# A two-layer attention kernel on one core: GELU values kept in the low half of their own slot, eight weight slots instead of six, and a start on host-transposed inputs

## The reference

```
# layer 0: only sequence 0's attention is used, and it is added to every sequence
q, k, v = x @ Wq0.T, ctx @ Wk0.T, ctx @ Wv0.T          # 16 heads
tgt2 = (softmax(q k^T / sqrt(32)) v)[0]
x = x + tgt2
# layer 1, for each of the 8 sequences
q = layer_norm(x; gq, bq) @ Wq ; k, v = layer_norm(ctx; gkv, bkv) @ Wkv
x = x + (softmax(q k^T * 32**-0.5) v) @ Wproj + bproj
x = x + gelu(layer_norm(x; gm, bm) @ W1 + b1) @ W2 + b2   # 512 -> 2048 -> 512, exact gelu
```

## Time and profile before

| what | value |
|---|---|
| median of 3 runs (lowest, highest) | 1812.53 us (1810.1, 1816.04) |
| the profiled execution, whole | 1814.68 us |
| its span, first to last instruction | 1812.9 us |
| mean granted TensorE clock | 0.987 of full speed |
| busy: PE, ACT, DVE, POOL | 95%, 64%, 60%, 52% of the span |

### The profile page before, as it was taken

The page is one execution under the profiler, slowest core; times in us unless marked ns, Lnnn a source line. Parts: engine busy times, 40 slices in busy tenths (PEclk is TensorE's granted clock), DMA queues, the critical chain, the costliest instruction groups (busy, mean ns, idle before and its releaser), DMA issues.

```text
span 1812.9 us, 23964 instructions
## 1 busy us (share of the span) xinstructions
PE 1724.4 (95%) x7488; PEld 1323.2 (73%) x7488; DVE 1083.6 (60%) x1860; ACT 1154.6 (64%) x1935; POOL 938.3 (52%) x802
## 2 busy tenths in 40 slices
PE   6899998998989899999999999999999999999898
PEld 5677776766666677777777777777777777777686
DVE  4566665477777566666665665666666656563322
ACT  3677764587877665766765576667657665874231
POOL 0454556157665464655555554646555545555241
PEclk8999999999999999999999999999999999999999
DMA  6688989675545575686666566756756675677262
GB/s 233 210 297 282 306 281 362 225 223 173 169 129 185 154 201 135 183 234 163 169 199 187 143 161 187 203 139 194 230 154 165 200 189 147 166 211 242 98 205 93
DMA packets 157102, 354.69 MB, mean 196 GB/s; under 512 B 29232, under 2 KB 47792, under 8 KB 156080
## 3 DMA queue, kind: packets, MB, share of 16 engines
q1 hardware_dynamic: 106096, 187.21, 35.5%
q10 hardware_dynamic: 50880, 165.95, 29.3%
HBM read 251.51 MB, written 82.08 MB: 184 GB/s over the span
## 4 chain that ended last, share of the span: by engine, by line
PE 69%; ACT 9%; issue 5%; DMA 5%; DVE 5%; POOL 4%; SPq 2%; ACTq 1%; DVEq 0%; POOLq 0%
PE ps_d L863 46%; PE ps_o L884 11%; PE ps_t L917 6%; PE ps_s L902 5%; DMA q_st<-negmax_t 2%; ACT p_hi L1026 1%; DMA rs<-o_raw 1%; ACT ps_t L1033 1%; ACT ps_d L937 1%; POOL p_lo L1288 1%; ACT ht L998 1%; PE ps_d L793 1%; DVE negmax L1176 1%; SPq L713 1%; DVE stats L1133 1%
## 5 line engine op out<-in xcount | busy, mean ns | idle before, releaser
L1288 POOL TENSOR_TENSOR p_lo<-p_full,p_hi 128x512 fp32r<-128x512 f32 x288 | 371.4, 1290 | 593.3 <-ACT p_full L1033 592.9
L1026 ACT ACTIVATE p_hi<-ps_t 128x512 fp32r<-128x512 f32 x576 | 345.3, 600 | 364.4 <-PE ps_t L917 359.6
L1176 DVE TENSOR_REDUCE negmax<-ps_s 128x1 fp32r<-128x512 f32 x576 | 389.2, 680 | 135.3 <-PE ps_s L902 134.9
L863 PE MATMUL ps_d<-hT,w_r 128*128 128x512 f32 x1536 | 422.1, 395 | 1.4 <-DVE hT L1081 1.3
L863 PE MATMUL ps_d<-w_r,g_s 128*128 128x512 f32 x1536 | 391.3, 394 | 5.5 <-DMA w_r<-w_scratch 5.5
L863 PEld LDWEIGHTS ps_d<-hT,w_r 128*128 128x128 f32 x1536 | 290.1, 190 | 74.0 <-DVE hT L1081 5.4
L863 PEld LDWEIGHTS ps_d<-w_r,g_s 128*128 128x128 f32 x1536 | 290.6, 190 | 71.2 <-issue 7.1
L1189 DVE TENSOR_TENSOR p_lo<-ps_t,p_hi 128x512 fp32r<-128x512 f32 x288 | 198.8, 690 | 232.2 <-ACT ps_t L1033 231.3
L917 PE MATMUL ps_t<-q_st,k_st 97*128 97x512 f32 x576 | 232.9, 404 | 17.3 <-DMA q_st<-negmax_t 12.1
L884 PE MATMUL ps_o<-p_hi,v_s 128*65 128x512 f32 x576 | 232.3, 403 | 12.6 <-POOL p_lo L1288 6.4
L902 PE MATMUL ps_s<-k_st,q_st 96*128 96x512 f32 x576 | 232.1, 403 | 5.3 <-DVE negmax L1176 5.0
(11 more groups left out here) (99 smaller groups left out, 2174.5 us busy)
## 6 DMA issues: line engine op xcount, KB each, us to landing
w_r<-w_scratch ACTq DMA_DIRECT2D x214, 512.0 KB, 4.9
w_r<-w_scratch SPq DMA_DIRECT2D x42, 512.0 KB, 4.7
v_scratch<-v_out SPq DMA_DIRECT2D x36, 520.0 KB, 5.1
k_scratch<-kq_out SPq DMA_DIRECT2D x36, 512.0 KB, 5.2
q_st<-q_scratch SPq DMA_DIRECT2D x144, 128.0 KB, 4.4
k_st<-k_scratch SPq DMA_DIRECT2D x144, 128.0 KB, 4.2
o_ab<-o_raw SPq DMA_DIRECT2D x144, 128.0 KB, 3.8
w_scratch<-piece_out SPq DMA_DIRECT2D x16, 1024.0 KB, 6.2
```

The source lines that it names most:

```text
L863: ins = nc.tensor.matmul(bank(u), lhs[a], rhs[b], start=(i == 0 and m == 0), stop=(i == 3 and m == 2))
L1026: act.activation(p_hi[:, c], ps_t[:, c % 2], ACT.Exp, scale=SCALE)
L1176: dve.tensor_reduce(negmax[:, h % 2, c:c + 1], ps_s[:, c % 2], AX.X, ALU.max, negate=True).then_inc(s_maxed, 1)
L1288: pool.tensor_tensor(p_lo[:, c], p_full[:, (by_gpsimd(s) - 1) % 2], p_hi[:, c].bitcast(F32), ALU.subtract).then_inc(p_pool_split, 1)
```

## The change

The identity and the transposes of the first two inputs leave the start: the host hands over `x0t` and `ctx0t` (sequence 0 of each, transposed), loaded in quarters into the still unused `v_s` and `q_st`; ACT and DVE make their halves directly. Of layer 0's key and query weights the 128 columns of the first unit come first, the value weights are split in four pieces, the other 384 columns come after them. `PRE` is 4 instead of 6, layer 1's first weights and block 0's first value tile come later in the order, and `xt0` is loaded only 40 ticks after the first score. In the MLP, `h_st` becomes two buffers that lie on the low halves of `g_s`'s two slots: GELU runs there in place, and POOL writes the low half over the value it came from. DVE's wait on `g_lo` goes. The 8 KB per partition that are freed make the ring of W2 eight slots. Block 1's first burst moves from tick +44 to +48 and gets the next two `hid` units as company.

```
-PRE = 6
+PRE = 4
-        for t, units in enumerate(([("a", 0, c) for c in range(FC)], [("a", 1, c) for c in range(FC)],
-                                   [("k", 0, 0)], [("q", 0, 0)], [("v", 0, 0), ("v", 0, 1)],
+        for t, units in enumerate(([("k", 0, 0)], [("q", 0, 0)], [("v", 0, 0), ("v", 0, 1)],
                                    [("v", 0, 2), ("v", 0, 3)])):
...
-                spread(range(at + 35, at + 44), turns + hidden(new, 0))
-                burst(at + 44, new, 0, [])
-                spread(range(at + 45, at + 55), hidden(new, 1))
+                spread(range(at + 35, at + 48), turns + hidden(new, 0))
+                burst(at + 48, new, 0, hidden(new, 1)[:2])
+                spread(range(at + 49, at + 55), hidden(new, 1)[2:])
...
-WHOLE_LOAD = {"wk": 0, "wv": PRE + 3, "wq": PRE + 11}
-WHOLE_HI = listed([(PRE + 1, "wk"), (PRE + 5, "wv"), (PRE + 14, "wq")])
+WHOLE_LOAD = {"wk": PRE - 1, "wv": PRE + 5, "wq": PRE + 11}
+WHOLE_HI = listed([(PRE + 3, "wk"), (PRE + 8, "wv"), (PRE + 14, "wq")])
...
-            values.append((max(at, max(PLAN.end("v", n, c) for c in range(TC)) + 1), (n, g)))
+            values.append((max(at, max(PLAN.end("v", n, c) for c in range(TC)) + (1 if n else 4)), (n, g)))
...
-W1_RING, W2_RING = 4, 6
+W1_RING, W2_RING = 4, 8
...
-    h_st = sb("h_st", [P, 4, T], F32)
+    h_st = [sb(f"h_st_{i}", [P, 4, T], F32, at=g_at + 4 * (2 * i + 1) * 4 * T) for i in range(2)]
...
+        def first_half(name, slot, raw):
+            for c in range(FC):
+                act.wait_ge(first_loaded[name][c], 16)
+                act.activation(aT[:, slot, 0, c], raw[:, c], ACT.Identity).then_inc(first_hi[name], 1)
...
-                done = GELU_NO[n, c // 4]
-                if done:
-                    dve.wait_ge(g_lo, 4 * done - 3 + c % 4)
                 dve.wait_ge(unit_ready, NO[u] + 1)
-                dve.tensor_scalar(h_st[:, c % 4], bank(u), col_s[:, 6 * FC + c:6 * FC + c + 1], None,
+                dve.tensor_scalar(hidden_of(n, c // 4)[:, c % 4], bank(u), col_s[:, 6 * FC + c:6 * FC + c + 1], None,
                                   ALU.add).then_inc(evacuated, 1)
...
-                pool.tensor_tensor(g_s[:, done % 2, 1, c], h_st[:, c], g_s[:, done % 2, 0, c].bitcast(F32),
+                pool.tensor_tensor(g_s[:, done % 2, 1, c], hidden_of(n, group)[:, c], g_s[:, done % 2, 0, c].bitcast(F32),
                                    ALU.subtract).then_inc(g_lo, 1)
```

More of the change, by code:

```diff
@@ L534, in xattn_program @@
     l0_loaded = {k: sem(f"{k}_loaded") for k in ("l0wk", "l0wq", "l0wv")}
+    l0_rest_loaded = {k: sem(f"{k}_rest_loaded") for k in ("l0wk", "l0wq")}
+    first_loaded = {k: [sem(f"{k}_loaded_{c}") for c in range(FC)] for k in ("ctx0t", "x0t")}
+    first_hi = {k: sem(f"{k}_hi") for k in ("ctx0t", "x0t")}
+    first_split = {k: sem(f"{k}_split") for k in ("ctx0t", "x0t")}
     whole_loaded = sem("whole_loaded")
@@ L612, in piece_in, with hidden_of @@
         return w2_raw[:, i % 2]
+    def hidden_of(n, group):
+        return h_st[GELU_NO[n, group] % 2][:]
     def source(kind, i):
@@ L627, in load_values @@
             queue.wait_ge(pv_done, (i - 1) * G * TC)
+        else:
+            queue.wait_ge(first_split["x0t"], FC)
         if g == 0:
@@ L700, in load_stack @@
                 sp.wait_ge(t_ready, (h - G) * TC + TC)
+            elif h == 0:
+                sp.wait_ge(first_split["ctx0t"], FC)
             if k == 0:
@@ L772, in _ @@
                 load_stage(sp, kind, b)
-            if tick == PRE:
+            if tick == PRE + 2:
                 load_stage(sp, "y", 1)
+            if tick == PRE + 40:
+                sp.dma_start(xt0[:], rows(x, 0)).then_inc(x0_loaded, 16)
             for name, at in WHOLE_LOAD.items():
@@ L990, in scaled @@
                 act.wait_ge(ln_shift, no + 1)
-                if (kind, i) == ("y", 0):
-                    act.wait_ge(unit_ready, ready("a", 0, FC - 1))
-                elif kind == "h" and i == 1:
+                if kind == "h" and i == 1:
                     act.wait_ge(wo_split, FC)
@@ L1001, in scaled, with l0_weights @@
                 ins.then_inc(normed, 1)
-        def l0_weights(name, dst, raw):
-            act.wait_ge(l0_loaded[name], 16)
-            act.activation(dst[:, 0], raw[:], ACT.Identity).then_inc(l0_hi, 1)
+        def l0_weights(loaded, hi, raw):
+            if loaded is not None:
+                act.wait_ge(loaded, 16)
+            act.activation(hi, raw, ACT.Identity).then_inc(l0_hi, 1)
+        def first_half(name, slot, raw):
+            for c in range(FC):
+                act.wait_ge(first_loaded[name][c], 16)
+                act.activation(aT[:, slot, 0, c], raw[:, c], ACT.Identity).then_inc(first_hi[name], 1)
+        l0_weights(l0_loaded["l0wk"], l0wk_s[:, 0, :, 0:P], l0wk_raw[:, :, 0:P])
+        first_half("ctx0t", 0, ctx0t_raw)
+        l0_weights(l0_loaded["l0wq"], l0wq_s[:, 0, :, 0:P], l0wq_raw[:, :, 0:P])
+        first_half("x0t", 1, x0t_raw)
         for tick in range(TICKS):
@@ L1016, in _ @@
                 act.wait_ge(evacuated, ready("hid", n, 4 * group + 3))
-                act.activation(h_st[:], h_st[:], ACT.Gelu).then_inc(gelu_done, 4)
+                act.activation(hidden_of(n, group), hidden_of(n, group), ACT.Gelu).then_inc(gelu_done, 4)
             s = PLAN.t_at.get(tick)
@@ L1063, in _ @@
             if tick == 0:
-                l0_weights("l0wk", l0wk_s, l0wk_raw)
+                for i in range(FC):
+                    l0_weights(None if i else l0_loaded["l0wv"], l0wv_s[:, 0, i], l0wv_raw[:, i])
             if tick == 1:
-                l0_weights("l0wq", l0wq_s, l0wq_raw)
-            if tick == 2:
-                l0_weights("l0wv", l0wv_s, l0wv_raw)
+                l0_weights(l0_rest_loaded["l0wk"], l0wk_s[:, 0, :, P:D], l0wk_raw[:, :, P:D])
+                l0_weights(l0_rest_loaded["l0wq"], l0wq_s[:, 0, :, P:D], l0wq_raw[:, :, P:D])
             for name in WHOLE_HI.get(tick, []):
```

95 lines of the change are left out of this document (57 added, 38 removed).

## The result

The changed kernel takes 1793.7 us (median of 4 runs, 1789.7 to 1796.27) against 1813.13 beside it: a ratio of 0.9891, 95% interval 0.9866 to 0.9916. It is faster by about 19.4 us. The forecast of 1781 (1771 to 1791) had the sign and missed the size: some 12 us of the expected 32 are not there. The profiled execution took 1793.32 us, its span is 1791.5.

The account below looks back on a forecast made before the run. PE, busy 95% of the span, was taken as the bound. Gains of 13.0 + 2 + 7.5 + 9.3 = 31.8 us from the profiled 1814.68 gave 1782.9, and 1781 for the median (range 1771 to 1791).

Parts of the forecast that it names:

- The start's 13.0: Program start: value matmuls begin at 15.2 instead of 28.2 us, 13.0 us won.
- my upper bound: Start: value matmuls at full clock would take 11 us instead of 14, for a gain of 16.
- the first rival: Start: the stack chain ends last, first score at 33, second score wins nothing; total 1787; chance 0.15.
- the 29.4 worked out: Start: when the stack's loads for the first score land, 29.4 us, beside 29.2 for the value matmuls.
- The rival by which the small loads land one after another: Start: ten small loads take 31 us instead of 6.2, 25 us lost, total 1806; chance 0.06.
- The rule that spoke against them: Split loads at the start: transfers should be 1 MiB or more; ten non-overlapping small loads 26 us, total about 1801.
- The first second score: First `ps_t`, behind the row of maxima: half a MB less ahead of it, 2 us won, between 0 and 5.
- The seven blocks between ... nothing is taken there: Blocks between block 1's burst and the tail: no wait found that touches `h_st` or W2, so no gain counted.
- The burst's 7.5: Block 1's first burst: 24 matmuls just cover the gap, removing 5.08 idle and 2.4 slow clock; 7.5 us won.
- The tail's 9.3: Tail: eight W2 slots remove PE's waits for W2 and the slow clock behind them; 9.3 us won, at least 5.5.
- forecast 31.8: Whole kernel: sum of the four gains, 13.0 + 2 + 7.5 + 9.3, taken from the profiled 1814.68 us.

Follow-up runs that it names:

- row_first: late_stage with the whole `wk` and the first value tile loaded behind the first row of maxima, and the halves of `wk` and `wv` later: 1805.73 us, ratio 0.9958.
- late_stage: The changed kernel with the first staged context tile, the identity and the constants loaded behind the second head's stack loads: 1793.57 us, ratio 0.9882.
- warm: The changed kernel with 55 idle matmuls, whose result nobody reads, ahead of eight instructions at which PE stood: 1784.70 us, ratio 0.9844.
- before_again: The kernel before the change, unedited, run once more for a second profile: 1807.89 us (one run).
- mlp_part: The kernel before with only the MLP part of the change (hidden values in `g_s`, eight W2 slots, later burst with two units): 1797.45 us, ratio 0.9913.
- warm_mlp: mlp_part (start of the kernel before) with idle matmuls in the same stalls as warm: 1796.97 us, ratio 0.9900.
- start_part: The changed kernel with the MLP part undone, so only the new start on the kernel before: 1806.71 us, ratio 0.9959.
- delay_4: The changed kernel behind a chain of four small loads of the identity, each waited for, ahead of the program: 1800.65 us, ratio 0.9918.

## Why the prediction missed

**The start's 13.0: nearly right in sum (12.2), by errors that partly cancel, which is luck.** Value matmuls came at 16.99, not 15.2: with ten small issues ahead on SP, `l0wv` is issued at 6.25 and lands 9.3 us later, at 15.55, not 13.8. But they ran at full clock, 11.41 us (my upper bound took 11). And the stack's chain ended last, by 1.58, as the first rival had it, at 29.98 for the 29.4 worked out (not at the rival's 33). The rival by which the small loads land one after another fell: the value weights are there 15.6 us into the span. The rule that spoke against them (the Trainium skill, DMA: Bandwidth & Descriptors, section Bandwidth) costs the 1.75 us named here at most, not the 20 by which its estimate in the forecast lay later; the page's figures are for loads issued from GpSimd, and these were issued by SP.

**The first second score: the first step that failed.** I forecast 2 us won and measured 2.2 lost. I counted what was taken away ahead of the row (half a MB) and not that the first context is now loaded twice, transposed and as it is. The bytes ahead of the second score are the same 15.5 MB. Nor did I count that the MB of `wk` went ahead of the first score before and goes behind it now, and I took the first value tile as new ahead of the row, where it already stood there (issued at 46.94, the row at 55.07). With `wk` and the tile behind the row the second score came 4.3 us sooner (`row_first` against `late_stage`). So the terms of 13.0 and 2 gave 10 together, and 9.5 were left at score 56.

**"The seven blocks between ... nothing is taken there": the step that cost most.** I let what is won at the first score count in full at the end and put the cost of the unchanged stalls behind it at what it was. Some 6.5 us of it go between scores 56 and 104: 2.6 more of idle time in the second stretch and 0.9 in the first, and 3 more of lost clock (7.6 for 4.5). The 2.6 is in part a low value of the first profile of before: its 10.23 of idle time were 11.31 and 12.00 in the two other profiles with the old start. `warm` shows that with the stalls filled nearly all that is there at score 56 comes through. Block 0 takes its share too: between scores 0 and 56, by the same reckoning, 2.7 to 7.5 us are lost to the clock with the new start, `warm` included (4.9), against 3.1, 1.6 and 1.6 in before, before_again and `mlp_part` (5.7 in `warm_mlp`). The Trainium skill, TensorE: Matmul & The Clock Gate, section "HAM oscillation — how this bites in real kernels", says that PE falls back to its lower clock where it waits between groups of matmuls. The traces agree in part (0.73 and 1.00 behind the same stall), and show that this can take back a gain won elsewhere.

**The burst's 7.5: right in mechanism, 1.1 short.** 6.4 in after, 7.1 in `mlp_part` (scores 160 to 184).

**The tail's 9.3: right in mechanism, 1.6 short in effect.** No wait for W2 is left, nor one for the later `xt0`. From 1660.44 to the end of the `out` units at 1684.95 and in the last 96 matmuls, 4.8 and 4.7 us are saved: 9.5. The half clock behind `ht` takes 1.6 back; it comes in `mlp_part` and `start_part` too, and not in `delay_4` or `row_first`. From score 568 to the end 7.7 are won in after, 9.4 in `warm`.

Of the forecast 31.8 the profile of after so lacks 5.5 up to score 56, 6.5 from there to 104, and 1.1 and 1.6 at the burst and in the tail; some 0.9 more goes in small steps, and the 5.2 between scores 320 and 328 are the stray of before's profile, which leaves the 21.4 by which the two profiles differ. `warm` takes 28.7 us less than the before that ran beside it (1813.36). That isn't the sum of 31.8 come true, as its idle matmuls also fill stalls that cost the kernel before half clock (4.5 us lost over the two stretches, 1.5 in `warm`).

**Open:** why the same stalls cost half clock more often behind the new start. The order of instructions is the same, and the moment is excluded by `delay_4`. One difference that goes with it is that SP's issue of an `o_ab` transfer 29.7 us after score 56 takes 1.2 to 1.6 us in the kernels with the new start but `row_first`, and 0.64 with the old start and in `row_first`; PE's next wait for POOL is 2.2 to 2.8 us for 1.1 to 1.6. But `row_first` loses 4.6 us to the clock between scores 56 and 64 all the same, so this alone isn't the cause. Why that issue takes longer I don't know, and three profiles with the old start are few.

## What to carry to other kernels

Microseconds won at the front of a program aren't won until they pass every later stall: read the granted clock behind each stall of the unchanged part, not only the waits of the changed one. Where PE must stand for one to three microseconds for work that can't come sooner, matmuls into a free bank cost nothing if they end before the wait does (0.19 and 0.32 us were left of it here) and can be worth more than a change of order; with the old start they were worth little. Of loads that are moved forward, count all bytes up to the next wait that matters, those that are now loaded twice too.

## What the runs showed of the hardware that I had not expected

- A stall of 2.03 or 3.05 us was followed by half clock in one kernel's execution and not in another's, though the instructions there are the same; in after a spell of it costs some 1.5 us of work (12 matmuls 4.45 and 4.60 us for 3.00 and 3.06).
- A 64 KB load at the program's start, issued and waited for alone, takes 1.7 us a time (four delay the first score by 6.85).
